# Shifted-window attention block: the weighed sum with 32 queries a weight on four column groups instead of 64 on two

## The reference

```
h   = layernorm(x) ; roll by (-4, -4) ; cut into 8 x 8 windows     # 512 windows of 64 positions
q, k, v = split(win @ qkv_w + qkv_b)                               # 4 heads of 16 channels
attn = softmax(q @ k.T * 16**-0.5 + bias + mask)                   # 64 x 64 for each window and head
out  = (attn @ v) @ proj_w + proj_b ; windows and roll undone
x    = x + out
x    = x + gelu(layernorm(x) @ fc1_w + fc1_b) @ fc2_w + fc2_b
```

## Time and profile before

| | us |
|---|---|
| runs shown, median of 3 (lowest, highest) | 501.47 (500.04, 504.29) |
| the profiled execution, its own time | 500.17 |
| its span in the trace | 498.4 |
| PE busy in the span | 436.9 |
| DVE busy in the span | 383.7 |
| POOL busy in the span | 378.2 |
| granted clock of PE, mean of the span | 0.985 |

### The profile page before, as it was taken

How to read it: one execution, slowest core, us unless ns; L and a number is a source line. 1 busy time by engine, 2 the same in 40 slices (tenths; PEclk the granted TensorE clock), 3 DMA queues, 4 the chain that set the end, 5 groups by cost and what they waited for, 6 DMA issues and landing times.

```text
span 498.4 us, 21474 instructions
## 1 busy us (share of the span) xinstructions
PE 436.9 (88%) x9630; PEld 329.1 (66%) x9630; DVE 383.7 (77%) x549; ACT 294.9 (59%) x437; POOL 378.2 (76%) x376
## 2 busy tenths in 40 slices
PE   0665978899999899999999999787999999999995
PEld 0542756687777777777777767675566676667664
DVE  2767697889999999899999989965467766777652
ACT  1233665675765665666657646543777677767761
POOL 2658989988988989989889799730588888888830
PEclk9995999999999999999999999999999999999999
DMA  8300523511411511511111101100011321330333
GB/s 166 68 1 22 130 64 69 122 30 26 118 34 26 125 29 24 130 25 27 41 26 35 35 24 31 39 3 3 3 40 49 87 59 30 87 78 11 87 90 81
DMA packets 9986, 27.10 MB, mean 54 GB/s; under 512 B 3368, under 2 KB 3368, under 8 KB 7976
## 3 DMA queue, kind: packets, MB, share of 16 engines
q1 hardware_dynamic: 9896, 25.74, 22.0%
HBM read 9.21 MB, written 8.39 MB: 35 GB/s over the span
## 4 chain that ended last, share of the span: by engine, by line
PE 71%; DMA 9%; ACT 8%; SPq 4%; issue 4%; DVE 2%; ACTq 0%; DVEq 0%
PE work L697 26%; PE outs L697 17%; PE scores L697 16%; DMA kX<-kT 5%; PE scores L798 5%; ACT kT L610 4%; PE scores L838 4%; SPq L283 3%; DMA params<-in_params 2%; ACT qT L612 2%; PE work L712 2%; DMA x<-in_x 1%; PE outs L826 1%; ACT probsT L645 1%; SPq L275 1%
## 5 line engine op out<-in xcount | busy, mean ns | idle before, releaser
L373 POOL TENSOR_TENSOR probs<-probs,negmax 128x1024 f32<-128x1024 f32 x64 | 123.8, 1934 | 27.2 <-DVE negmax L489 27.1
L339 POOL TENSOR_TENSOR stat_rstd<-stat_var,minus_half 128x8 f32<-128x8 f32 (+1 forms) x62 | 104.9, 1691 | 5.0
L483 DVE TENSOR_TENSOR probs<-scores,bias 128x1024 f32<-128x1024 f32 x64 | 77.9, 1217 | 14.2 <-PE scores L697 14.2
L645 ACT ACTIVATE probsT<-scores 128x1024 f32<-128x1024 f32 x64 | 65.6, 1025 | 28.8 <-PE scores L798 28.8
L344 POOL TENSOR_TENSOR xn<-x,stat_mean 128x256 f32<-128x256 f32 (+1 forms) x91 | 78.1, 876 | 4.1
L697 PE MATMUL outs<-vX,probsT 128*64 128x34 f32 x2048 | 72.2, 225 | 9.4 <-issue 8.3
L489 DVE TENSOR_REDUCE negmax<-probs 128x16 f32<-128x1024 f32 x64 | 78.1, 1220 | 2.2
L697 PEld LDWEIGHTS outs<-vX,probsT 128*64 128x64 f32 x2048 | 65.9, 138 | 19.1 <-issue 19.0
L697 PEld LDWEIGHTS work<-params,probs 128*64 128x64 f32 x2048 | 62.3, 138 | 23.5 <-DVE x L577 20.5
L798 PEld LDWEIGHTS scores<-ident,probs 128*128 128x128 f32 x512 | 55.5, 142 | 28.1 <-issue 24.2
L610 ACT ACTIVATE kT<-work,bqkv 128x512 f32<-128x512 f32 x31 | 21.3, 688 | 86.6 <-PE work L697 86.6
(11 more groups left out here) (61 smaller groups left out, 662.4 us busy)
## 6 DMA issues: line engine op xcount, KB each, us to landing
kX<-kT SPq DMA_DIRECT2D x124, 64.0 KB, 2.0
x<-in_x SPq DMA_DIRECT2D x32, 224.0 KB
out<-x SPq DMA_DIRECT2D x28, 224.0 KB
x<-in_x SPq DMA_DIRECT2D x32, 32.0 KB
out<-x SPq DMA_DIRECT2D x28, 32.0 KB
out<-x SPq DMA_DIRECT2D x16, 56.0 KB
params<-in_params SPq DMA_DIRECT2D x1, 805.5 KB, 12.0
out<-x SPq DMA_DIRECT2D x16, 8.0 KB
```

The lines of the kernel that those rows point to most:

```text
L339: nc.gpsimd.tensor_tensor(stat_rstd[:, cols], stat_var[:, cols], minus_half[:, cols], ALU.pow).then_inc(ln_rstd, pieces)
L373: nc.gpsimd.tensor_tensor(e, e, top, ALU.add).then_inc(shifted, 1)
L483: nc.vector.tensor_tensor(e[:, :].rearrange("q (u a m) -> q a u m", u=2, a=2), scores[k].rearrange("q (a u m) -> q a u m", a=2, u=2), b.re ...
L645: nc.scalar.activation(probsT[n % 2][:, :], trans, ACT.Exp)\
```

## The change

The loop over the two windows' column halves (64 queries each) becomes a loop over four runs of 32 queries. Each product has 32 stationary columns instead of 64, and writes 32 output partitions instead of 64; the moving operand is the same 34 columns and is now used four times for each `u` and `h` where it was used twice. Output, waits and the signal are the same.

```
                 for u in range(2):
                     for h in range(HEADS):
-                        for w in range(2):
-                            at = (u * HEADS + h) * P + (w ^ k) * N
+                        for rows in range(0, P, 32):
+                            w = rows // N
+                            at = (u * HEADS + h) * P + (w ^ k) * N + rows % N
                             row = (w * 4 + 2 * k + u) * HEADS + h
-                            out = outs[w * N:(w + 1) * N, u * HEADS * VW:(u + 1) * HEADS * VW]\
+                            out = outs[rows:rows + 32, u * HEADS * VW:(u + 1) * HEADS * VW]\
                                 .rearrange("q (p h d) -> q p h d", p=2, h=HEADS)[:, :, h]
-                            done = mm(out, probsT[n % 2][:, at:at + N], vX[image % 2][:, row, :])
+                            done = mm(out, probsT[n % 2][:, at:at + 32], vX[image % 2][:, row, :])
                 done.then_inc(outs_ready, 1)
```

## The result

The changed kernel takes 510.5 us (median of 4 runs, 508.4 to 517.2) beside 500.8 for the kernel before: a ratio of 1.021, 95% interval 1.012 to 1.031. The forecast was 491.2 us: the sign was wrong. The profiled execution took 510.83 us with a span of 509.0.

A forecast was written before the change was run, and what follows sets the result against it. PE, busy 88% of the span, was taken as the bound, with DVE equally full in the middle stretch. Landed savings of 2.5 + 4.4 + 2.9 + 0.5 = 10.3 us gave 491.2 us beside the median; range 485 to 501.

The forecast's parts named there:

- What one burst costs: Weighed sum on PE: a burst takes 1.06 us, its 58.4 ns round set by the 64-column load, not streaming.
- Step (c), issue: Issuing 64 pairs a burst: between 0.53 and 0.84 us; 0.70 taken behind the scores, upper end behind a wait.
- What lands: Attention stage, stage by stage: of 18.2 us gross, 10.3 us shorten the kernel, since PE's bursts loop with other engines.
- Rival 4, instruction fetch: PE's instruction queue: 16 more packets, at 1.31 us each 21 us against the gain, some 512 us; chance 0.04.
- Rivals 1 and 2: Weigh's bursts: two column groups at a time, 501 us, chance 0.12; or 29.2 ns a pair, 553 us, chance 0.08.
- Rival 3: Attention stage: bursts shrink, but DVE or the keys' DMAs absorb the saving, 498 us; chance 0.13.
- What would show it: Signs in the new profile: bursts of 0.65 to 0.95 us, DVE idle about 10 us less; one sign for each rival.

The follow-up runs named there:

- half of the queries: The changed kernel computing only queries 0 to 31 of each window after the first half image: 486.6 us, ratio 0.972 to the kernel before.
- the variant with the most holes: The changed kernel with the weighed sum of odd steps moved behind the QK fill and the transposes: 535.2 us, ratio 1.066 to the kernel before.

## Why the prediction was wrong

**What one burst costs** was right. The load of 64 columns set the round of 58.4 ns, and with 32 columns it is 33 ns (half of the queries: 16.6 ns a pair in two groups). In four groups a pair takes (0.77 - 0.196) / 63 = 9.1 ns, a round 36 ns. The forecast bursts of 0.70 and 0.84 us came out as 0.69 and 0.78.

**Step (c), issue,** asked the right question and bounded it by the wrong thing. I took 13.2 ns a pair as the upper end for issue within one burst. Within a burst it is at least as fast as 9.1 ns. The limit that counts is on a block of 256 records: about 14.7 ns a record, 29.4 ns a pair, averaged over more than one burst. No single burst of the kernel before shows it, since a burst is shorter than a block. The sum of what lands has no term for it.

**What lands** was right in size: 10.3 of 18.2 us, 57%, were forecast; 52% landed in the run without added records (14 of 27 us). By stage its trace, a slower execution than the median, is 2.0 us ahead at 121 us, 5.5 us at 286 us and 9.2 us at the start of the MLP stage (338.4 beside 347.6): 0.7 us a group in the middle stretch, where the forecast had about 1, and 3.7 of 13 x 0.42 = 5.5 us at the end, which is less whole than the forecast's 2.9 of 3.6. In the changed kernel the bursts save 32 x 0.37 + 32 x 0.28 = 21 us gross; at the same share 11 to 12 us land, and the 21.4 us of added holes turn that into a loss of 10. This last sum is an argument from shares, not a measurement: how much of each hole lands wasn't taken apart, and the half clock isn't in it.

**Rival 4, instruction fetch,** is what happened, at a chance of 0.04 and with some 512 us as its time, which is near the result. The failing step is there: the forecast puts late instructions at nothing, because "that V fill is the only burst I found broken so, against 76 packets", and takes 16 added packets at 1.31 us as the most that they could cost. The reading was incomplete: the V fill at 80.11 us is torn too. And both sentences price a late block as an accident that comes with a packet. The runs showed that the price isn't by the packet: with the same 16 added packets the holes came to 17.7, 23.7, 29.8 and 38.8 us, by the order and the length of the bursts. That 16 x 1.31 = 21 us lies beside 21.4 us of added holes, and 512 beside 510.5, is luck.

What decides is the time of each block. 14 of the 19 holes, 14.5 of 23.7 us, stand behind packets that began less than 2 us after the block ahead; in 12 of these cases PE had got through that block in 3.3 us or less. The other five stand behind packets that began late, which is nearer to the accident of rival 4; ahead of the largest of them the block had kept PE busy for only 2.7 us. The kernel before shows only that second kind. Its hole at 99.12 is no measurement of the rate, but the count between it and the one at 80.11, 2497 - 1728 = 769 records, three blocks and one record, would have shown the blocks. The question then is how much of a block's 5.35 us the change takes away, against the some 3.76 us that the next one needs.

**Rivals 1 and 2** are refuted: four column groups do stream side by side, and a pair of full height can cost 9.1 ns. The floor of about 25 ns from start to start that the prediction names from the Trainium skill, "TensorE: Matmul & The Clock Gate", section "Wait — 56ns, not 53.3ns?", doesn't hold here either: these pairs start 9.1 ns apart. Rival 3 is refuted by the half of the queries.

**What would show it** worked: the holes "of a microsecond inside bursts" were named there for rival 4.

## What to carry to other kernels

Shortening a product's array time by cutting it into more matmuls also multiplies instructions, and PE's instructions have a limit of their own, here 256 records in about 3.8 us where blocks are late in a row. Before such a cut, look for bursts torn for 1 to 2 us with "issue" as the reason, and count the records between two of them: a multiple of 256 says that the next block of instructions wasn't there. It doesn't say why. For that, look at how long PE took over the block ahead, and at when the next packet began. Then count in blocks, not over the stage: the average lay under the supply in all four kernels for which it is given here, and the variant with the most holes had 55 records a us. Look at the granted clock behind long holes. Measure each reordering in both versions, because a move that seems to spread instructions may gain or lose by quite another path.

## What the runs showed that I had not expected

- Bursts torn between two blocks of 256 records: 19 holes with 23.7 us in the changed kernel, 36 with 38.8 us in the worst variant, all at 192 or 193 modulo 256, ending 1.2 to 1.6 us after a 16 KB packet landed.
- Half of a loss can come from one place: a hole of 4.07 us, with 6.8 us at 1.2 GHz behind it, put the changed kernel back by 5.3 us within one image.
- Where two blocks in a row are late, supply sets a pace of about 14.7 ns a record. Within a burst the weighed sum goes through a record in 4.6 ns (9.1 ns a pair), three times as fast.
- Matmuls of 34 columns in four column groups start 9.1 ns apart with weights of full height.
- A larger sum of holes doesn't mean a slower kernel across variants: with the QK fill ahead, holes rose from 23.7 to 29.8 us while the time didn't grow (1.0105 beside 1.021).
- Removing 1024 records in the V fills didn't reduce the holes (25.3 us), and the fills became longer by 0.42 us; which places help wasn't settled.
